# State-space phase: one PSUM sum for both directions and the skip term, a transform read from normalized rows, and a softplus split by direction

## The reference, cut to what matters

```python
xz = einsum('bld,ed->bel', hidden_states, in_proj_w)            # hidden_states: the normalized x
out = branch(xz, ...)                                           # forward
out_b = branch(xz[:, :, ::-1], ...)                             # backward
# branch: x, z = split(xz); x = silu(causal_conv(x) + bias); dt, Bm, Cm = parts of x_proj @ x
#   delta = softplus(dt_proj @ dt + bias);  h_l = exp(delta*A) * h_(l-1) + delta*Bm*x
#   y = (sum over states of h*Cm + Dp * x) * silu(z)
xf = fftn(x of xz, axes=(-2, -1)); xc = silu(conv5(concat(real, imag)) + bias)
v = abs(ifftn(complex(re, im)) * max_l(silu(z))); out_f = (v - mean) / sqrt(var + 1e-05)
result = einsum('bdl,od->blo', out + out_b[:, :, ::-1] + out_f, out_proj_w)
```

## Time and profile before

| what | value |
|---|---|
| median of three runs | 2189.67 us |
| the profiled execution: its own time | 2191.28 us |
| its span | 2189.5 us |
| granted TensorE clock, mean | 0.957 |
| TensorE busy | 2025.2 us, 92% |
| VectorE busy | 1706.0 us, 78% |
| ScalarE busy | 1375.2 us, 63% |
| GpSimd busy | 1116.2 us, 51% |
| state-space phase | from about 1370 to 2118 us |

### The profile page before, as it was taken

One profiled execution on the slowest core, in us unless ns is written; L12 is line 12 of the kernel. 1 busy time (PEld: TensorE's weight loads), 2 busy tenths in 40 slices (PEclk: granted clock), 3 DMA queues, 4 the chain that ended last, 5 costly groups with the idle time before them and its releaser, 6 DMA issues. The chain is left out here.

```text
span 2189.5 us, 40536 instructions
## 1 busy us (share of the span) xinstructions
PE 2025.2 (92%) x14572; PEld 1505.7 (69%) x14572; DVE 1706.0 (78%) x2956; ACT 1375.2 (63%) x2686; POOL 1116.2 (51%) x1509
## 2 busy tenths in 40 slices
PE   6999999986999996999999979699999999999878
PEld 5677777755888873777777646486686776876746
DVE  5777777766888876777777766499999999999964
ACT  1677777763777773777777653558567576676533
POOL 3555555614776665555555403264655646646323
PEclk8999999997999997999999989799999999999979
DMA  4665565630000004555555513000000000000000
GB/s 132 151 148 148 144 152 146 149 89 0 2 1 2 1 1 107 152 148 147 152 144 149 135 50 153 1 1 1 1 1 1 1 1 1 1 1 1 1 15 20
DMA packets 147750, 144.94 MB, mean 66 GB/s; under 512 B 14048, under 2 KB 106976, under 8 KB 146912
## 3 DMA queue, kind: packets, MB, share of 16 engines
q1 hardware_dynamic: 127968, 132.91, 22.3%
q10 hardware_dynamic: 19584, 9.44, 2.3%
HBM read 94.07 MB, written 38.80 MB: 61 GB/s over the span
## 5 line engine op out<-in xcount | busy, mean ns | idle before, releaser
L606 DVE TENSOR_REDUCE sb_f_mx<-ps_f_s 128x2 f32<-128x512 f32 x768 | 505.9, 686 | 216.3 <-PE ps_f_s L354 215.2
L530 ACT ACTIVATE sb_f_pt<-ps_f_t 128x1024 f32<-128x1024 f32 x384 | 382.2, 1023 | 114.3 <-issue 56.2
L1941 POOL TENSOR_TENSOR sb_mb_h<-sb_mb_h 128x512 f32<-128x512 f32 x128 | 164.7, 1308 | 322.8 <-DVE sb_mb_h L1809 322.3
L354 PE MATMUL ps_f_s<-sb_f_stack 96*128 96x256 bf16 x1536 | 287.2, 280 | 20.5 <-DMA sb_f_stack<-f_scr 12.9
L1804 DVE TENSOR_TENSOR_SCAN sb_mb_h<-sb_mb_da,sb_mb_h 128x1024 f32<-128x1024 f32 x128 | 300.8, 2388 | 4.3 <-ACT sb_mb_da L1681 4.3
L1517 PE MATMUL ps_mb_f<-sb_mb_fc,sb_mb_cw 128*128 128x256 f32 x1280 | 286.1, 380 | 2.8 <-ACT sb_mb_fc L1694 2.8
L1517 PEld LDWEIGHTS ps_mb_f<-sb_mb_fc,sb_mb_cw 128*128 128x128 f32 x1280 | 239.7, 190 | 35.7 <-ACT sb_mb_fc L1694 3.0
L1681 ACT ACTIVATE sb_mb_da<-sb_mb_dl,sb_mb_an 128x255 f32<-128x255 f32 x512 | 211.6, 495 | 42.9 <-DVE sb_mb_h L1804 39.6
L371 PE MATMUL ps_f_t<-sb_f_stack 128*128 128x256 bf16 x1536 | 232.4, 273 | 5.9 <-ACT sb_f_pt L530 3.3
L354 PEld LDWEIGHTS ps_f_s<-sb_f_stack 96*128 96x128 bf16 x1536 | 140.6, 99 | 108.8 <-issue 42.2
L427 PE MATMUL ps_f_a<-sb_f_pt,sb_f_v 128*32 128x256 f32 x3072 | 187.7, 385 | 1.6 <-ACT sb_f_v L579 1.6
(11 more groups left out here) (253 smaller groups left out, 4164.2 us busy)
## 6 DMA issues: line engine op xcount, KB each, us to landing
f_scr<-sb_f_parts SPq DMA_DIRECT2D x96, 384.0 KB, 2.7
sb_f_stack<-f_scr SPq DMA_DIRECT2D x192, 192.0 KB, 3.0
sb_f_stack<-f_scr SPq DMA_DIRECT2D x192, 128.0 KB, 3.1
sb_f_stack<-f_scr SPq DMA_DIRECT2D x192, 64.0 KB, 3.3
sb_f_stack<-sb_f_mrow ACTq DMA_DIRECT2D x96, 96.0 KB
sb_mb_cw<-in_cw SPq DMA_DIRECT2D x1, 5120.0 KB, 19.2
sb_prep_wn<-in_wn SPq DMA_DIRECT2D x6, 512.0 KB, 7.2
sb_m_w<-in_w SPq DMA_DIRECT2D x6, 256.0 KB, 3.3
```

The lines of the kernel that those rows point to most:

```text
L354: last = nc.tensor.matmul(s_bank[j % 2][:, h, :], stack[0:ROWS, a.n % STACKS, 0, g * GROUP + pair * 2 + h, half * P:(half + 1) * P], stack ...
L530: nc.scalar.activation(pt[:, e.two, g, half, :, :], t_bank[i % 2][:, :, :], ACT.Exp).then_inc(s["pt_sb"], 1)
L606: nc.vector.tensor_reduce(mx[:, a.two, half, head:head + 2], s_bank[j % 2][:, :, :], AX.X, ALU.max)\
L1941: nc.gpsimd.tensor_tensor(hb[:, c, 0:2, :], hb[:, c, 0:2, :], hb[:, c, 2:4, :], ALU.add).then_inc(s["half_sb"], 1)
```

## The change

One sum: `total` now adds all eight units of a sequence into `y_bank`, the backward ones through an output that runs backwards over the positions. A new function `direct` adds the skip term to the same bank with a diagonal matrix `dd` (made once, by ScalarE, in slot 3 of the first sequence, from the identity and `dp`): two matmuls in slot 6 and two in slot 7. `collect`, the reversed sum and their semaphores are gone, and `gather` is one product of `y_bank` with `sz`. `total` of unit 0 waits for that product (`ym_sb`), `total` of unit 4 for nothing but its input. `xc` has two buffers instead of three, and its writer waits for `direct`.

The transform over positions (the former L1496) reads the normalized rows `ny`, now a tile of its own for all eight sequences. The transposition, the copy to `xt` and the guard in GpSimd's `fetch` are gone; the squares count up `f_sb` one by one, and the transform waits for the first.

First sequence: the softplus of the forward direction is issued after its bias in slot 4, that of the backward one in slot 6, and VectorE's `dl` and `dx` are split likewise. The product that makes `gw` (`combine`) and its copies move from ahead of the steps into the step in which the first sequence is scanned: on TensorE at its head, on ScalarE behind the decays of unit 0.

```diff
+    dd = w.gm[:, 1, :, :].rearrange("p t n -> p (t n)")[:, 0:2 * DC * P].rearrange("p (r c n) -> p r c n", r=2, c=DC)
...
-        xc = k.sb("mb_xc", [P, 3, 2, DC, N], ctx)
+        xc = k.sb("mb_xc", [P, 2, 2, DC, N], ctx)
...
-        yr = k.sb("mb_yr", [P, DC, N], ctx)
-        xt = k.sb("mb_xt", [P, 2, D], ctx)
...
-        ny = e[:, :, :, :].rearrange("p r c (i n) -> p (r c) i n", i=2)
+        ny = k.sb("mb_ny", [P, B, 2, D], ctx)
...
-                if slot == 0 and half == 0:
+                if slot == 0 and half == 1:
                     if m.b == 0:
                         pe.wait_ge(s["gw_sb"], 2)
-                    def positions(o):
-                        for l in range(2):
-                            last = nc.tensor.transpose(o[:, l * D:(l + 1) * D], xb[:, m.parity, EDGE + l * P:EDGE + (l + 1) * P],
-                                                       k.ident[:, :])
-                        return last
-                    turn(0, 0, positions)
-                elif slot == 0 and half == 1:
+                    since(pe, "f_sb", seen - 1)
+                    for l in range(2):
+                        last = nc.tensor.matmul(f_bank[1][:, :], ny[:, m.b, l, :], fa[:, l, :], start=l == 0, stop=l == 1)
+                    last.then_inc(s["f_ps"], 1)
+                elif slot == 0 and half == 2:
                     pe.wait_ge(s["f_sb"], seen + 1)
-                    def dft_l(o):
-                        for l in range(2):
-                            last = nc.tensor.matmul(o[:, :], xt[:, l, :], fa[:, l, :], start=l == 0, stop=l == 1)
...
-                    turn(1, 1, dft_l)
-                elif slot == 0:
-                    pe.wait_ge(s["f_sb"], seen + 2)
...
-                        pe.wait_ge(s["f_sb"], seen + 4)
+                        pe.wait_ge(s["f_sb"], seen + 3)
...
                 r, g = divmod(un, SU)
                 n = m.b * UNITS + un
                 pe.wait_ge(s["hs_sb"], DC * (n + 1))
-                if g == 0 and r == 0:
-                    since(pe, "yr_sb", m.b)
-                elif g == 0:
-                    pe.wait_ge(s["yf_sb"], m.b + 1)
+                if un == 0:
+                    since(pe, "ym_sb", m.b)
                 for c in range(DC):
-                    last = nc.tensor.matmul(y_bank[:, c, :], k.ident[:, :], h[:, n % HBUFS, c, 0, :],
-                                            start=g == 0 and c == 0, stop=g == SU - 1, skip_group_check=True)
+                    last = nc.tensor.matmul(y_bank[:, c, ::1 - 2 * r], k.ident[:, :], h[:, n % HBUFS, c, 0, :],
+                                            start=un == 0 and c == 0, stop=un == UNITS - 1, skip_group_check=True)
                 last.then_inc(s["y_ps"], 1)
+
+            def direct(m, r):
+
+                if m.b == 0:
+                    pe.wait_ge(s["dd_sb"], 1)
+                for c in range(DC):
+                    last = nc.tensor.matmul(y_bank[:, c, ::1 - 2 * r], dd[:, r, c, :], xc[:, m.parity, r, c, :],
+                                            start=False, stop=False, skip_group_check=True)
+                if r:
+                    last.then_inc(s["dd_ps"], 1)
...
+            def combine():
...
             def step(f, m, o):
+                if m and m.b == 0:
+                    combine()
...
                         total(o, UNITS - 2 + slot)
                     if m and slot == 6:
                         total(m, slot - 2)
+                        direct(m, 0)
                         spread(m, slot, 1)
...
+                    if m and slot == 7:
+                        direct(m, 1)
...
-            for part in range(2):
...
-                    since(act, "yr_sb", f.b - 2)
+                    since(act, "dd_ps", f.b - 1)
...
-            def softplus(f):
...
-                act.wait_ge(s["u_sb"], 2 * f.b + 2)
-                since(act, "dl_sb", f.b)
-                nc.scalar.activation(e[:, :, :, :], dl[:, f.parity, :, :, :], ACT.Abs).then_inc(s["abs_sb"], 1)
...
+            def softplus(f, rs):
+
                 if f.b == 0:
+                    inc, n, need = 1, rs.stop, rs.stop
+                else:
+                    inc, n, need = 2, 2 * f.b + 2, 2 * f.b + 2
+                act.wait_ge(s["u_sb"], need)
+                since(act, "dl_sb", 2 * f.b)
+                nc.scalar.activation(e[:, rs, :, :], dl[:, f.parity, rs, :, :], ACT.Abs).then_inc(s["abs_sb"], inc)
+                act.wait_ge(s["abs_sb"], n)
+                nc.scalar.activation(e[:, rs, :, :], e[:, rs, :, :], ACT.Exp, scale=-1.0).then_inc(s["exp_sb"], inc)
+                if f.b == 0 and rs.start == 0:
...
                 if un == 0:
-                    act.wait_ge(s["dl_sb"], m.b + 1)
+                    act.wait_ge(s["dl_sb"], 1 if m.b == 0 else 2 * m.b + 2)
+                if un == SU and m.b == 0:
+                    act.wait_ge(s["dl_sb"], 2)
...
                     for dc in range(DC):
-                        last = nc.scalar.activation(sq[:, dc, :], f_bank[(1 + dc) % 2][:, :], ACT.Square)
-                    last.then_inc(s["f_sb"], 1)
...
-            def transposed(m):
-                act.wait_ge(s["f_ps"], m.b * FREQ + 1)
-                nc.scalar.activation(xt[:, :, :].rearrange("p l c -> p (l c)"), f_bank[0][:, 0:2 * D], ACT.Copy)\
-                    .then_inc(s["f_sb"], 1)
+                        nc.scalar.activation(sq[:, dc, :], f_bank[(1 + dc) % 2][:, :], ACT.Square).then_inc(s["f_sb"], 1)
...
                 if m:
-                    transposed(m)
                     decay(m, 0, range(1, DC))
+                if m and m.b == 0:
+                    act.wait_ge(s["gw_ps"], 1)
+                    nc.scalar.activation(gw[:, 0:2, :].rearrange("p t n -> p (t n)"), f_bank[0][:, :], ACT.Copy).then_inc(s["gw_sb"], 1)
+                    nc.scalar.activation(gw[:, 2, :], f_bank[1][:, 0:CH_I], ACT.Copy).then_inc(s["gw_sb"], 1)
...
+                    if m and m.b == 0 and slot == 3:
+                        for r in range(2):
+                            for c in range(DC):
+                                last = nc.scalar.activation(dd[:, r, c, :], k.ident[:, :], ACT.Copy, scale=dp[:, r, c:c + 1])
+                        last.then_inc(s["dd_sb"], 1)
+                    if f and f.b == 0 and slot == 4:
+                        softplus(f, slice(0, 1))
                     if f and slot == 6:
-                        softplus(f)
+                        softplus(f, slice(1, 2) if f.b == 0 else slice(0, 2))
...
+            def steps(f, rs):
+
+                if f.b == 0:
+                    inc, n = 1, rs.stop
+                else:
+                    inc, n = 2, 2 * f.b + 2
+                dve.wait_ge(s["ln_sb"], n)
...
+                dve.wait_ge(s["dl_sb"], n)
...
-                if slot == 7:
...
+                if slot == 4 and f.b == 0:
+                    dve.wait_ge(s["an_exp"], 1)
+                    nc.vector.tensor_scalar(an[:, :, :, :], an[:, :, :, :], -1.0, None, ALU.mult).then_inc(s["consts"], 1)
+                    steps(f, slice(0, 1))
+                elif slot == 7:
+                    steps(f, slice(1, 2) if f.b == 0 else slice(0, 2))
...
-            def collect(m, r):
-
-                dve.wait_ge(s["y_ps"], m.b * UNITS + (r + 1) * SU)
-                if r == 0:
-                    since(dve, "o_ps", m.b - 1)
-                dst = (ys[:, m.parity, :, :], yr)[r]
-                for c in range(DC):
-                    last = nc.vector.scalar_tensor_tensor(dst[:, c, :], xc[:, m.third, r, c, :], dp[:, r, c:c + 1],
-                                                          y_bank[:, c, :], ALU.mult, ALU.add)
-                last.then_inc(s[("yf_sb", "yr_sb")[r]], 1)
-
...
-                collect(o, 1)
-                dve.wait_ge(s["yr_sb"], n)
-                nc.vector.scalar_tensor_tensor(yf[:, :, :], yf[:, :, :], 1.0, yr[:, :, ::-1], ALU.mult, ALU.add)\
-                    .then_inc(s["ysum_sb"], 1)
-                dve.wait_ge(s["ysum_sb"], n)
-                nc.vector.scalar_tensor_tensor(yf[:, :, :], yf[:, :, :], 1.0, sz[:, o.parity, :, :], ALU.mult, ALU.mult)\
-                    .then_inc(s["ym_sb"], 1)
+                dve.wait_ge(s["y_ps"], UNITS * n)
+                since(dve, "o_ps", n - 2)
+                nc.vector.tensor_tensor(yf[:, :, :], y_bank[:, :, :], sz[:, o.parity, :, :], ALU.mult).then_inc(s["ym_sb"], 1)
...
-                    if m and slot == SU + 2:
-                        collect(m, 0)
...
-                since(pool, "f_ps", (b - 2) * FREQ + 1)
```

72 lines of the change are left out of this document (30 added, 42 removed).

## The result

The changed kernel takes **2170.2 us** (median of four runs, 2167.5 to 2171.6) against 2189.6 of the kernel before (four runs beside them): a ratio of **0.9904**, 95% interval 0.9892 to 0.9917. The forecast was 2164.3 with a range of 2156 to 2180, so sign and range hold, and 5.9 us of the forecast gain did not come. The two profiled executions stand at 2169.9 and 2191.28 us, with spans of 2168.1 and 2189.5; the state-space phase went from 748.54 to 727.16 us, which is all of the 21.4, and what lies outside it is 1440.9 in both.

What follows compares the result with a forecast made beforehand. VectorE and TensorE were nearly full; afterwards a loop through both sets 84.4 us periods. Start -0.7, periods -15.8, last sequence -7.3, tail -1.6: -25.4, from profiled 2191.28 to 2165.9, less 1.6 for the median: 2164.3 us, range 2156 to 2180.

Steps and rivals of the forecast that it cites:

- Own work of the engines: Each engine's time per sequence without its waits, after the change: VectorE 82.8 us, TensorE 83.2 us.
- The product: VectorE's single 128x512 product of PSUM and `sz` replacing the old `gather` of 3.17 us: 0.68 us, bounds 0.42 and 1.2.
- Two thirds of what VectorE drops is given back: The steady period falls only 2.75 us, from 87.1 to 84.4, much less than the work VectorE loses.
- Loop B: Product with `sz`, first `total`, TensorE's work to `project_out`, VectorE's output addition, next period: 84.4 us, the longest, setting the period.
- Loop A: From the squares over ScalarE to the `yk` copy (8.1 us), then TensorE to the next squares (75.9): 84.0 us.
- Six periods: Sequence 1 to sequence 7: first period 85.0, then five of 84.4, 507.0 us against 522.8, a gain of 15.8.
- First sequence: Start of the phase: first scan 3.5 us earlier, first transform delayed by the `gw` copies, sequence 1 starts 0.7 us earlier.
- Last sequence and tail: Last sequence loses VectorE work and the 4.08 us wait before the output addition, -7.3 us; tail shrinks to one product, -1.6.
- rival 1: TensorE's reversed PSUM writes cost up to 0.22 us more per row: 2183 us; at three times the row 2211; chance 0.13.
- rival 2: TensorE's clock falls in the new, shorter gaps, costing 1.5 us a period: 2174 us; chance 0.12.
- rival 3: VectorE's change works only in part: `ym` late more often or GpSimd's half sums late, 1 us a period: 2171; chance 0.15.
- rival 4: The loop through the `sz` product is looser than laid out and TensorE's own 83.2 us rules: 2157 us; chance 0.15.

Runs made afterwards that it cites:

- better version: Changed kernel with three moves: strengths' scaling behind the `fc` copies, skip-term products at the next step's start, weight product inside the front step; 2161.1 us, 0.9859.
- sum alone: Kernel before with only the single PSUM sum of both directions and skip term; transform, softplus and weight product unchanged; 2184.2 us, 0.9964.
- dead work: Changed kernel with VectorE products added whose result nothing reads, in two runs: 6.4 us per sequence, 2210.0 us; 3.7 us per sequence, 2179.4 us.
- second dead-work run: Changed kernel with four unread 256-element VectorE products ahead of each sequence's seventh scan, 3.7 us, none before the gate's product; 2179.4 us, 0.9949.

## Why the prediction came out as it did

**Own work of the engines: right.** TensorE: 84.77 less its gaps (0.19, 0.49, 0.42) and three drains of 0.16 is 83.2, as forecast; the better version gives 84.19 - 0.72 - 0.32 = 83.15. VectorE: 84.77 - 1.60 = 83.2 against 82.8. The product took 0.67 for 0.68. "Two thirds of what VectorE drops is given back" holds in kind: two engines bound together, as the sum alone and the dead work show.

**The period: the wrong loop, nearly the right length.** The step that failed is that Loop B, 84.4, is the longest. The row of the first total has no gap, and the product 0.66 us earlier changed nothing. Its terms were right: 20.6 to the product's end, 49.1 from the total to the output addition, 14.6 from there (1755.48 to 1776.06, 1776.62 to 1825.68, 1825.68 to 1840.24), 84.2 in all, which leaves the 0.56 us between product and total. What bounds is loop C, 84.77, which I didn't lay out: it shares loop B's way to `project_out` and over VectorE, but leaves VectorE earlier, at `zo`, and comes back to TensorE over the scaling and the `fc` copies. Loop A was put at 84.0: squares to `yk` 8.1 is right (1750.81 to 1758.93), but L1492 to the squares takes 76.6 (1758.98 to 1835.57) instead of 75.9, since loop C's wait of 0.42 for `fc`, with its drain, lies in it; without that wait loop A is 84.42. Moving the scaling took 0.35 off. That the forecast is off by only 0.4 us is in part luck: three loops lie within 0.6 us of each other. Six periods from sequence 1 on fell from 522.8 to 509.3, 13.6 instead of 15.8: 2.2 us of the miss.

**First sequence: rows put at their usual length, and two large effects that cancel.** I forecast 0.7 earlier; sequence 1 starts 0.1 later after the phase's start (127.07 before, 127.19 after). The first scan comes 2.7 earlier (41.31 for 44.05), forecast 3.5. As forecast the transform then waits for the `gw` copies and starts 0.8 behind that scan (0.9), and the convolution behind it is 1.2 early (1.0). I had not counted that its rows would take 4.69 instead of 3.62 after 4.18 us of standing: L1492 is only 0.1 early (49.48 for 49.61), and that is the miss. What the move costs as a whole I didn't see at all. Without it and the split, the second `yk` comes 126.46 us after the start instead of 130.52: the two halves are worth 4.1 there, since the wait of 7.30 in front of the first transform goes as well, where I gave the missing transposition 0.27. The move costs 5.4 of it. The split is worth 0.75, forecast 0.65. That so little was left to miss is luck.

**Last sequence and tail.** -6.8 for -7.3 and -1.1 for -1.6; the last total still waits 3.34 us for GpSimd's half sum, and its rows then take 2.07 at the low clock, which I had not counted. Together with the periods (2.2) and the start (0.8) these 1.0 make the 4.0 us between 25.4 and 21.4; the other 1.9 of the 5.9 is scatter of the totals: the profiled execution lay 1.6 above its median before and 0.3 below it after.

**Rivals.** Reversed writes cost nothing (rival 1). The clock didn't fall in the new gaps in the middle sequences (rival 2); in the first and last sequence it did, behind waits of 3.3 us and more. GpSimd wasn't late in a steady sequence (rival 3). TensorE's own work (rival 4) is not the bound: the better version is still 1.0 us above it.

## What to carry to other kernels

Where two engines are within 2 us of each other per round, price a change on both, and walk the new round through every queue: the copy that TensorE waited for stood behind a small pair of instructions that the copy doesn't need, and these waited for VectorE. Where several loops are within 1 us of each other, cutting the longest brings only the distance to the next: 0.35 here for a loop, 0.58 for all three moves. A one-time product moved out of the way belongs where nobody waits for it: its place was worth 8 us, over a third of what the whole change brought. Small effects are better read from equal periods in a profiled execution than from totals.

## What the runs showed of the hardware

A PSUM output with a step of -1, 2 or -2 fp32 elements cost the matmuls here nothing: 1.02 to 1.03 us for four rows each time, and the VectorE product that reads such a tile took 0.67 in both layouts. The Trainium skill, "PSUM — Partial Sum Buffer", Specifications, says that a non-contiguous access pattern slows matmuls significantly; for fp32 outputs of 256 columns these runs disagree.

VectorE's scans take 4.46 us a pair in some slots and up to 5.40 in others of the same sequence, and GpSimd's rows beside the long ones are stretched too. GpSimd of the kernel after:
```profile
1797.71 2.66 POOL L1959 TENSOR_TENSOR sb_mb_bcr<-sb_mb_bcf,sb_mb_bc 128x256 f32<-128x256 f32 x1
...
1817.02 2.67 POOL L1959 TENSOR_TENSOR sb_mb_bcr<-sb_mb_bcf,sb_mb_bc 128x256 f32<-128x256 f32 x1
```
The shortest of its sixteen takes 0.67. In the second dead-work run the later one took 0.86 (1819.71 to 1820.57, beside the last dead product and VectorE's L1815), and the scans that ran beside it in the kernel after 4.46 instead of 5.40. The Trainium skill, "GPSIMD Engine Reference", Specifications, says that GpSimd shares its SBUF interface with VectorE and that they contend when a VectorE instruction has two SBUF inputs, as the scan has; the trace agrees, with 0.94 us on a pair of scans (5.40 for 4.46). That this sharing is the cause was not tested by itself.

TensorE's clock: with no wait above 0.5 us in a period the granted clock stayed at 1.00 (2.4 GHz) in five periods running; after waits of 2.4 to 4.2 us the rows behind ran long in some cases and not in others (2.56 and 1.98 behind two waits of 2.4; 4.69 for 3.62 at a granted clock of 0.79).
